# A first chunk on four PSUM banks, sums cleared by GpSimd, and input transfers issued by SyncE

## What is computed

```
x = x + L0_attn(norm(x)); x = x + mLSTM(norm(x), ctx); x = x + experts(norm(x))
x = x + L1_attn(norm(x)); x = x + cross_attention(ctx, norm(x))
# the last block, h = norm(x), 64 experts of 32 slots = 2048 slots
logits = einsum('bmd,dnp->bmnp', h, phi)
dispatch = softmax(logits, axis=0)            # over the sequences
combine = softmax(logits over all n*p)        # over the slots
slots = einsum('bmd,bmnp->bnpd', h, dispatch)
y = slots @ W + b
out = x + einsum('bnpd,bmnp->bmd', y, combine)
```

## Time and profile before

| | us |
|---|---|
| median of three runs | 2063.2 |
| the profiled execution: its own time | 2060.2 |
| its span | 2058.1 |
| PE busy | 1863.2 (91%) |
| DVE busy | 1458.5 (71%) |
| ACT busy | 1446.9 (70%) |
| POOL busy | 1123.8 (55%) |
| loading | 0 to about 50 |
| soft mixture | about 1330 to 2058 |

### The profile page before, as it was taken

One profiled execution on the slowest core, in us unless ns is written; L12 is line 12 of the kernel. 1 busy time (PEld: TensorE's weight loads), 2 busy tenths in 40 slices (PEclk: granted clock), 3 DMA queues, 4 the chain that ended last, 5 costly groups with the idle time before them and its releaser, 6 DMA issues. The chain is left out here.

```text
span 2058.1 us, 62588 instructions
## 1 busy us (share of the span) xinstructions
PE 1863.2 (91%) x23443; PEld 1475.0 (72%) x23505; DVE 1458.5 (71%) x3895; ACT 1446.9 (70%) x4203; POOL 1123.8 (55%) x1453
## 2 busy tenths in 40 slices
PE   5899798699999998889879999767999999999998
PEld 3566565577777776566568888656888888888787
DVE  7799768666566665677756666578777777777567
ACT  5688767688888887688768888566666666666532
POOL 5677447688888888545333333147444544445520
PEclk9999999899999999899999999899999999999999
DMA  3011010322222222000011111100000000000101
GB/s 98 28 48 41 13 33 3 83 73 73 74 72 77 73 73 62 23 2 2 2 34 32 33 33 33 58 26 4 5 15 18 5 16 5 16 15 3 56 8 39
DMA packets 60619, 72.47 MB, mean 35 GB/s; under 512 B 10264, under 2 KB 38696, under 8 KB 60064
## 3 DMA queue, kind: packets, MB, share of 16 engines
q1 hardware_dynamic: 51104, 64.29, 10.5%
q10 hardware_dynamic: 9216, 4.20, 0.7%
HBM read 51.43 MB, written 4.44 MB: 27 GB/s over the span
## 5 line engine op out<-in xcount | busy, mean ns | idle before, releaser
L1094 POOL TENSOR_TENSOR ff_hl<-ff_hid,ff_hh 128x512 fp32r<-128x512 f32 x272 | 350.2, 1302 | 69.1 <-ACT ff_hh L1335 61.9
L1954 POOL TENSOR_TENSOR sm_zsum<-sm_zsum,sm_logits 128x512 f32<-128x512 f32 x120 | 154.6, 1289 | 271.2 <-ACT sm_logits L1980 269.5
L1257 DVE TENSOR_TENSOR ff_hid<-ff_p_b,ff_gates 128x512 f32<-128x512 f32 x240 | 164.4, 686 | 148.6 <-ACT ff_p_b L1324 146.4
L1997 ACT ACTIVATE sm_sT<-sm_p_s 128x512 f32<-128x512 f32 x128 | 69.5, 595 | 217.3 <-PE sm_p_s L1790 217.3
L613 ACT ACTIVATE at_pr<-at_p_s,at_small 128x64 f32<-128x64 f32 x512 | 154.9, 329 | 61.1 <-DVE at_small L499 61.1
L1335 ACT ACTIVATE ff_hh<-ff_hid 128x512 fp32r<-128x512 f32 x272 | 169.9, 625 | 39.1 <-DVE ff_hid L1257 38.9
L1324 ACT ACTIVATE ff_p_b<-ff_p_h,early_b 128x512 f32<-128x512 f32 x240 | 156.9, 654 | 19.3 <-PE ff_p_h L1151 18.0
L1966 POOL TENSOR_TENSOR sm_logits<-sm_logits,sm_peak 128x512 f32<-128x512 f32 x128 | 163.1, 1296 | 12.5 <-ACT sm_comb L2015 11.9
L1804 PE MATMUL sm_p_l<-g_phi,g_xnT 128*128 128x256 f32 x512 | 142.3, 404 | 26.5 <-ACT sm_logits L2025 25.3
L582 POOL TENSOR_TENSOR at_kblk<-at_kT,early_heads 128x512 f32<-128x512 f32 x128 | 131.7, 1049 | 28.9 <-PE at_p_s L479 26.7
L1838 PE MATMUL sm_p_y<-sm_w,sm_sT 128*32 128x128 f32 x4096 | 125.4, 274 | 9.1 <-ACT sm_combT L1987 8.4
(11 more groups left out here) (305 smaller groups left out, 5610.1 us busy)
## 6 DMA issues: line engine op xcount, KB each, us to landing
ff_gates<-kept_gates SPq DMA_DIRECT2D x120, 256.0 KB, 3.1
xa_kturn<-xa_ksin SPq DMA_DIRECT2D x128, 64.0 KB, 2.0
at_turned<-at_terms SPq DMA_DIRECT2D x64, 64.0 KB, 1.9
sm_w<-in_w_soft SPq DMA_DIRECT2D x8, 512.0 KB, 3.5
early_whole<-in_L_ffn_rW SPq DMA_DIRECT2D x30, 128.0 KB, 2.6
early_xs<-in_x ACTq DMA_DIRECT2D x32, 64.0 KB, 1.9
ld_ctx<-in_ctx ACTq DMA_DIRECT2D x32, 64.0 KB, 2.1
x_kept<-early_xs SPq DMA_DIRECT2D x1, 2048.0 KB, 7.4
```

The lines of the kernel that those rows point to most:

```text
L1094: eng.tensor_tensor(hl[:, q, :], hid[:, q, :], hh[:, q, :].bitcast(F32), ALU.subtract).then_inc(h_split, 1)
L1257: dve.tensor_tensor(h, p_b[c % 2][:, :], gates[:, n % GR, :], ALU.mult).then_inc(scaled, 1)
L1954: pool.tensor_tensor(z, z, logits[:, j % RING_L, :, :], ALU.add).then_inc(summed, 1)
```

## The change

In loading, SP issues all transfers of x and ctx: tiles 0 and 1, then the three constants, then the tiles from 2 on, from tile 8 with the waits that ACT had; the ten weights of the next stage go one at a time behind the tiles 8, 10, ... 26. ACT issues none. In the mixture the units 2, 3, 6, 7, 10, 11, 14, 15 of the first chunk have their logits in `p_y` in place of `p_l`, so PE waits for the copy of unit j-4 there; the first two transposes of combine wait for the copies of the units 14 and 15. `acc` is cleared by GpSimd, and DVE waits for that before its first update of `acc`.

```diff
         def _(sync):
+            def load(t):
+                sync.dma_start(g["xs"][:, t, :], x_d[t]).then_inc(x_in[t % R], 16)
+                sync.dma_start(ctx[:, t % R, :], c_d[t]).then_inc(c_in[t % R], 16)
+
+            for t in range(2):
+                load(t)
             for dst, src in loads:
                 sync.dma_start(dst, src).then_inc(consts_in, 16)
-            at["in"].load(sync, at["loads"][0])
+            for t in range(2, NT):
+                if has(t - R):
+                    sync.wait_ge(transposed, t - R + 1)
+                    sync.wait_ge(normed, 2 * (t - R + 1))
+                load(t)
+                if t >= R and t % 2 == 0:
+                    at["in"].load(sync, at["loads"][0][(t - R) // 2:(t - R) // 2 + 1])
...
-            for t in range(R - 1):
-                load(t, t)
-
             def turn(t, u):
-                if has(t + R - 1):
-                    if has(t - 1):
-                        act.wait_ge(transposed, t)
-                        act.wait_ge(normed, 2 * t)
-                    load(t + R - 1, (u + R - 1) % R)
...
+        def bank_l(j):
+
+            return (p_y if j < UNITS and j // 2 % 2 else p_l)[j % 2]
...
-                            if j > 1:
+                            if 4 <= j < UNITS:
+                                pe.wait_ge(l_copied, j - 3)
+                            elif j >= UNITS:
                                 pe.wait_ge(l_copied, j - 1)
...
                             if j > 1:
                                 pe.wait_ge(turn_copied, j - 1)
+                            else:
+                                pe.wait_ge(l_copied, UNITS - 1 + j)
...
+                    if j == 0:
+                        dve.wait_ge(acc_cleared, 1)
...
-                dve.memset(acc[:, :, :], 0.0).then_inc(set_up, 1)
...
-                dve.wait_ge(set_up, 3)
+                dve.wait_ge(set_up, 2)
...
+                pool.memset(acc[:, :, :], 0.0).then_inc(acc_cleared, 1)
```

More of the change, by code:

```diff
@@ L208, in _ @@
             act.wait_ge(consts_in, 16 * len(loads))
[L210 to L214, removed]
-            for t in range(R - 1):
-                load(t, t)
-            def turn(t, u):
-                if has(t + R - 1):
-                    if has(t - 1):
-                        act.wait_ge(transposed, t)
-                        act.wait_ge(normed, 2 * t)
-                    load(t + R - 1, (u + R - 1) % R)
+            def turn(t, u):
                 act.wait_ge(transposed, t + 1)
@@ L1693, in soft_experts @@
         phi_in, w_in = m.sems("phi_in", 2), m.sems("w_in", 2)
-        set_up, xt_done, xt_copied = m.sem("set_up"), m.sem("xt_done"), m.sem("xt_copied")
+        set_up, acc_cleared, xt_done, xt_copied = m.sem("set_up"), m.sem("acc_cleared"), m.sem("xt_done"), m.sem("xt_copied")
         l_done, row_maxed, topped, l_copied = (m.sem(n) for n in ("l_done", "row_maxed", "topped", "l_copied"))
@@ L1803, in _ @@
                                 t = u * TU + a
-                                mm = pe.matmul(p_l[h][:, a * CW:(a + 1) * CW], xnT[:, t * P:(t + 1) * P], phi[:, c % 2, :], start=True, stop=True)
+                                mm = pe.matmul(bank_l(j)[:, a * CW:(a + 1) * CW], xnT[:, t * P:(t + 1) * P], phi[:, c % 2, :], start=True, stop=True)
                             mm.then_inc(l_done, 1)
@@ L1898, in _ @@
                         c, u = parts(j)
-                        both = p_l[j % 2][:, :].rearrange("p (a s) -> p a s", a=TU)
+                        both = bank_l(j)[:, :].rearrange("p (a s) -> p a s", a=TU)
                         dve.wait_ge(l_done, j + 1)
@@ L2024, in _ @@
                             act.wait_ge(s_done, j - RING_L + 1)
-                        act.activation(logits[:, j % RING_L, :, :].rearrange("p a s -> p (a s)"), p_l[j % 2][:, :], ACT.Copy).then_inc(l_copied, 1)
+                        act.activation(logits[:, j % RING_L, :, :].rearrange("p a s -> p (a s)"), bank_l(j)[:, :], ACT.Copy).then_inc(l_copied, 1)
 def program(nc, io, out):
```

## The result

The changed kernel took 2051.05 us, median of 5 runs (2047.73 to 2051.83), the kernel before, timed with it, 2063.45 (5 runs, 2062.44 to 2070.49). By the medians that is 12.4 us or 0.6% faster; the ratio estimated over all the runs is 0.9928, 95% interval [0.9911, 0.9945], or 11.3 to 18.4 us. The forecast was 2050.7. On another chip it took 2047.38 against 2060.02, ratio 0.9935 [0.9921, 0.9949]. The profiled execution took 2051.35 us with a span of 2047.4.

A forecast was written before the change was run, and what follows sets the result against it. Bound: DVE's pace in loading after a late start, and PE and DVE waiting for each other over two banks in the mixture's first chunk. Terms -2.9, -3.7 and -5.9 us: 2063.2 - 12.5 = 2050.7 us, range 2047.3 to 2055.7.

The forecast's parts named there:

- Loading: First stage: tile 2's statistics start at 6.7 against 9.63, lasting to the stage's end; -2.9 us, ends -1.5 and -3.3.
- a sign of being wrong: Loading: the prediction is wrong if DVE waits for `xs` or `ctx` behind tile 8; no size given.
- Rival 3: Loading: SP can't keep up issuing, at 0.98 us each 22.9 us late, total 2073.6; 0.03 with any other slowdown.
- The clearing: Mixture's start: clearing `acc` moves to POOL, 3.8 us hidden in its idle time; DVE's first maximum 2.5 us earlier.
- the hold of 0 to 1 us: Mixture's start: DVE's clearing of `yy` might be held until POOL's clearing ends, costing 0 to 1 us.
- The third step: Mixture's first chunk: DVE's third step starts 3.7 us earlier, ends -2.3 and -5.1, the clearing's 2.5 us within it.
- Five steps: Mixture's first chunk: with four banks five steps take 12.1 us in place of 18.03; -5.9 us, ends -6.0 and -5.0.
- Rival 1: Mixture: something besides the banks, ACT's copies or late logits, sets the step's pace; 2055.1 us, chance 0.11.
- Does it last?: Mixture after the first chunk: the gain stays whole, though clock dips may cost or save up to 1.5 us.
- rival 2: Mixture: the pipeline's filling absorbs the banks' gain, only loading's is left; 2060.3 us, chance 0.06 with other ways to within 4.1.
- The sum: Whole kernel: the terms of loading, third step and five steps add to 12.5 us faster, 2050.7 us.

The follow-up runs named there:

- load_only: The kernel before with only the change's loading, the mixture as before; 2060.60 us against 2062.74, ratio 0.9984.
- act_first: The kernel before, with ACT issuing its first 14 transfers before it waits for the constants; 2058.87 us against 2062.73, ratio 0.9984.
- pool_decay: The changed kernel with the difference of maxima (decay) computed by GpSimd instead of DVE; 2049.64 us, ratio to the kernel before 0.9940.
- the second profile: The changed kernel run again, unedited, on another chip; 2047.38 us against 2060.02 for the kernel before, ratio 0.9935.
- clear_only: The kernel before with GpSimd clearing `acc`, logits still on two banks and loading as before; 2059.83 us against 2062.74, ratio 0.9980.
- gap_kept: The changed kernel, but logits of units 2 and 3 wait for copies of units 0 and 1 as with two banks; 2047.37 us, ratio to before 0.9935.
- sp_consts_first: The kernel before with loading issued by SP alone, but the three constants ahead of tiles 0 and 1; 2056.68 us against 2060.02, ratio 0.9982.

## Why the prediction was right, step by step

- **Loading**, forecast -2.9, measured -2.4 and -1.8 in the changed kernel and -3.0 in load_only. Tile 2 came at 6.58 (forecast 6.7), with the landing time of 2.1 us chosen there: 2.0 in the changed kernel's transfers of 5 to 8. The 3.1 us of the earlier trace rows wasn't ACT's queue's own: in the kernel before its transfers landed in 1.9 to 2.0 us from 12 on, when SP had nothing left to issue, and in act_first in 3.9 to 4.1 while both issued (3 to 6). A wait of DVE for `xs` behind tile 8 was named as a sign of being wrong, and it came, at tile 27, by 0.51 and 0.93 us. The working took landing as a constant 2.1 us; x27 was asked for at 33.56 and landed in 4.3, behind a repeated weight that took 4.6. That the weight delayed it is how the rows read; no run moved the weight alone.
- **Rival 3**, SP as the bound, didn't occur, but its mechanism is real: seven issues for two tiles cost 8.3 us. An issue took 0.475 us in loading, below the 0.52 from which it was to cost. The margin is 0.1 us for two tiles.
- **The clearing**: 3.54 us on POOL (forecast 3.8), hidden with 19.22 us of idleness behind it. `yy` beside it was not held (0.07 us), so the hold of 0 to 1 us was 0. The first maximum came 2.16 us behind the first logits in place of 4.50, near the 2.5 us that were forecast, but on top of the banks only 1.6 us of it last to the third step.
- **The third step**, forecast -3.7 between -2.3 and -5.1, measured -5.2, just outside. This is the term that was mis-sized most. The forecast took the middle between a low and a high clock for PE's second group; it ran at the high one in every kernel with four banks. Its other side moves as well: the old mixture took 11.58 to 13.35 us here, 12.94 in the profile that the forecast started from, so a part of the 1.5 us is where the clock rose in that one.
- **Five steps**, forecast -5.9 at 2.42 us each, measured -6.07 at 2.39: four DVE operations of 0.60 with no idle time. PE needs 2.17 and runs ahead. Rival 1 is out: neither ACT's copies nor late logits set the pace.
- **Does it last?** Forecast as whole. The first chunk ended 13.6 us earlier (12 to 13 were named), but 1.2 us are given back by the second chunk's end, in both profiles, mostly (0.85) to a DVE operation that now fell beside a busy POOL; pool_decay shows that such a hold reaches the path. That is not rival 2's absorption, which would have left only loading. The prediction looked for holds in the first steps alone, not where the new timing would put DVE's small operations against POOL's. The 1.67 us in the table's last line can't be put down to the change: the second profile has 0.26 there, and the other kernels 627.8 to 630.2 us for the same part, those with the old mixture 627.8 to 629.2.
- **The sum**, 12.5 us forecast and 12.4 by the medians, was off by 0.1 because errors cancelled: +1.5 at the third step and +0.2 in the steps against -0.5 to -1.1 in loading and -1.2 at the second chunk; the interval is 7 us wide besides. The mechanisms were right; that closeness is luck.

## What to carry to other kernels

When two engines each wait for the other in turn with nothing else as releaser, count the buffers between them: a step then costs the slower engine's own time, which can be read from the trace before the edit. In a stage's start, ask what the first useful transfer waits for before asking who issues it, and when issues are merged into one queue, leave room for the slowest landing, not only for the issue rate. Price a small operation by what its neighbour does at the new time, not by the duration that it had.

## What had not been expected of the hardware

- Three small DVE operations in a row beside a busy GpSimd took 1.0 to 1.5 us each, in place of 0.2 to 0.4; not the first alone was held.
- A 64 KB transfer that repeats one row to all partitions landed after 3.8 to 4.6 us (load_only, the changed kernel), and those right behind it after 3.5 to 4.3, among transfers with a median of 2.4.
- PE's clock did not fall in a pause of 1.18 us (clear_only, gap_kept), but was low for the third group of load_only behind a pause of the same 1.18 us. The pause ahead of its second group, 1.86 us, doesn't explain it either: sp_consts_first had the same two pauses, and its third group was fast (1.99 us). What sets the clock at the stage's start stays open.

```profile
1332.13 2.32 PE L1800 MATMUL sm_p_l<-g_phi,g_xnT 128*128 128x256 f32 x8 [1.86 <-ACT sm_logits L2021]
...
1336.07 1.99 PE L1800 MATMUL sm_p_l<-g_phi,g_xnT 128*128 128x256 f32 x8 [1.18 <-ACT sm_logits L2021]
```
